# GpSimd rounds the rows in the first pass of the last feed-forward; VectorE keeps only the maxima

## The reference, cut to what matters

```
def quant_act_uint8(x):
    s = max(max(x), EPS) / 255.0            # one scale for the whole tensor
    return clip(round(x / s), 0, 255) * s, s

def quant_linear(x, w, b):                  # weights: int8, one scale per output row
    xq, s_in = quant_act_uint8(x)
    return xq @ wq.T + round(b / (s_in * s_w)) * (s_in * s_w)

x = x + quant_linear(relu(quant_linear(layernorm(x), w1, b1)), w2, b2)
```

## Time and profile before

| | |
|---|---|
| median of 3 executions | 2360.57 us (2360.05 to 2366.0) |
| profiled execution, its own time | 2361.02 us |
| span of its profile | 2359.2 us |
| TensorE busy | 2286.8 us, 97% |
| VectorE busy | 1743.7 us, 74% |
| ScalarE busy | 1587.5 us, 67% |
| GpSimd busy | 1691.7 us, 72% |
| first pass, first round to last maximum | 2250.78 to 2292.59 us |
| from there to the end of the span | 66.6 us |

### The profile page before, as it was taken

One profiled execution on the slowest core, in us unless ns is written; L12 is line 12 of the kernel. 1 busy time (PEld: TensorE's weight loads), 2 busy tenths in 40 slices (PEclk: granted clock), 3 DMA queues, 4 the chain that ended last, 5 costly groups with the idle time before them and its releaser, 6 DMA issues.

```text
span 2359.2 us, 62966 instructions
## 1 busy us (share of the span) xinstructions
PE 2286.8 (97%) x20874; PEld 1830.5 (78%) x20874; DVE 1743.7 (74%) x4342; ACT 1587.5 (67%) x4467; POOL 1691.7 (72%) x1863
## 2 busy tenths in 40 slices
PE   7999999999999999999999999999999999999788
PEld 6778877778788777778877778787777878877546
DVE  5777777787777777777777777777778777778785
ACT  6666666776667677666766766666677666667356
POOL 2777777777777777777787777777777777877607
PEclk9999999999999999999999999999999999999899
DMA  4000000000000000000000000000000000001202
GB/s 147 10 11 10 10 8 10 2 10 10 10 10 9 10 2 10 10 10 10 10 8 9 4 10 10 10 10 8 10 2 10 10 10 10 8 4 36 57 11 63
DMA packets 31472, 37.06 MB, mean 16 GB/s; under 512 B 3301, under 2 KB 29653, under 8 KB 31445
## 3 DMA queue, kind: packets, MB, share of 16 engines
q1 hardware_dynamic: 31444, 36.71, 5.3%
HBM read 29.36 MB, written 7.34 MB: 16 GB/s over the span
## 4 chain that ended last, share of the span: by engine, by line
PE 88%; DVE 4%; ACT 4%; issue 3%; POOL 2%; DMA 0%; POOLq 0%; ACTq 0%; SPq 0%; DVEq 0%
PE ps L367 25%; PE pt L471 11%; PE ps L447 10%; PE pa L483 7%; PE pt L461 5%; PE ps L411 5%; PE pa L523 4%; PE pa L498 4%; ACT probT L828 3%; PE ps L435 2%; PE pa L367 2%; PE pt L367 2%; PE pa L633 1%; PE ps L426 1%; DVE th L1547 1%
## 5 line engine op out<-in xcount | busy, mean ns | idle before, releaser
L1145 DVE TENSOR_REDUCE nmx<-ps 112x2 f32<-112x750 f32 x512 | 478.2, 934 | 142.2 <-PE ps L447 91.4
L1643 POOL TENSOR_TENSOR prob<-prob,rinv 112x375 f32<-112x375 f32 x512 | 404.2, 810 | 130.3 <-DVE rinv L1153 130.2
L1643 POOL TENSOR_TENSOR prob_last<-prob_last,rinv 112x375 f32<-112x375 f32 x512 | 411.9, 830 | 59.1 <-DVE rinv L1153 59.0
L828 ACT ACTIVATE room<-ps 128x376 f32<-128x376 f32 (+2 forms) x480 | 227.5, 487 | 265.9 <-PE ps L367 265.9
L828 ACT ACTIVATE probT<-pt 125x336 f32<-125x336 f32 (+1 forms) x512 | 242.6, 474 | 167.8 <-PE pt L461 112.5
L868 ACT ACTIVATE prob<-ps,nmx 112x375 f32<-112x375 f32 x512 | 289.9, 581 | 65.0 <-DVE nmx L1145 65.0
L868 ACT ACTIVATE prob_last<-ps,nmx 112x375 f32<-112x375 f32 x512 | 290.7, 584 | 8.2 <-DVE nmx L1145 8.2
L1670 POOL TENSOR_TENSOR krs<-krs,nhalf 125x48 f32<-125x48 f32 x32 | 257.0, 8030 | 0.0
L1136 DVE COPY probT<-pt 125x336 f32<-125x336 f32 x322 | 161.9, 503 | 97.4 <-PE pt L471 97.3
L483 PE MATMUL pa<-probT,room 125*64 125x112 f32 x3072 | 183.0, 265 | 0.0
L471 PEld LDWEIGHTS pt<-ident,prob 112*125 112x125 f32 x966 | 118.5, 189 | 72.7 <-issue 64.2
(11 more groups left out here) (294 smaller groups left out, 5981.0 us busy)
## 6 DMA issues: line engine op xcount, KB each, us to landing
craw<-in_ctx SPq DMA_DIRECT2D x32, 375.0 KB, 3.1
xin<-in_x SPq DMA_DIRECT2D x32, 112.0 KB, 2.0
x_rows<-x SPq DMA_DIRECT2D x32, 112.0 KB, 1.9
out<-probT SPq DMA_DIRECT2D x16, 224.0 KB, 2.3
room<-x_rows SPq DMA_DIRECT2D x1, 2576.0 KB, 13.7
w<-in_f1w SPq DMA_DIRECT2D x2, 1024.0 KB, 6.6
stage<-in_wk SPq DMA_DIRECT2D x2, 512.0 KB, 4.7
stage<-in_wv SPq DMA_DIRECT2D x1, 1024.0 KB, 7.5
```

The source lines that it names most:

```text
L828: return act.activation(dst, src, ACT.Copy)
L1145: top = dve.tensor_reduce(nmx[:, g:g + 2], ps[0:T, 2 * (i % 2):2 * (i % 2) + 2, 0:S], AX_X, ALU.max, negate=True)
L1643: pool.tensor_tensor(prob(i, n), prob(i, n), rinv[:, g:g + 1].to_broadcast([T, S]), ALU.mult).then_inc(s["normed"], 1)
```

## The change

The eight roundings leave VectorE's program and stand in GpSimd's, in one loop in front of the waits for the second pass. Each keeps its two waits, its operands, its operation and its counter. VectorE's program of the first pass is then the bias operations and 32 maxima in order. The waits of TensorE and ScalarE are unchanged.

```diff
-            def round_rows(c):
-                dve.wait_ge(s["xn3_ready"], c * CH + CH)
-                dve.tensor_scalar(xq3, x3n, ROUND, ROUND, ALU.add, ALU.subtract).then_inc(s["xq3_ready"], 1)
...
-            round_rows(0)
             link(dve.tensor_scalar(t8[:, 4, 0:FC], t8[:, 6, 0:FC], t8[:, 13, 0:1], None, ALU.mult))
             link(bias(t8[:, 4, 0:FC], f1b1[:], FC, t8[:, 5, 0:FC]))
-            def next_rows(c):
-                dve.wait_ge(s["xq3T_ready"], c + 1)
-                round_rows(c + 1)
-
             for c in range(NCH):
-                if 0 < c < NCH - 1:
-                    next_rows(c)
                 largest(c, 0)
                 largest(c, 1)
-                if c == 0:
-                    next_rows(c)
                 largest(c, 2)
                 largest(c, 3)
...
             pool.tensor_tensor(mr[:, B - 1:B, 1], mr[:, B - 1:B, 1], nhalf[0:T, 0:1], ALU.pow).then_inc(s["rstd3"], 1)
+            for c in range(NCH):
+                if c >= 1:
+                    pool.wait_ge(s["xq3T_ready"], c)
+                pool.wait_ge(s["xn3_ready"], c * CH + CH)
+                pool.tensor_scalar(xq3, x3n, ROUND, ROUND, ALU.add, ALU.subtract).then_inc(s["xq3_ready"], 1)
             pool.wait_ge(s["row_sb"], 2)
             pool.wait_ge(s["xq3_ready"], NCH)
```

## The result

The changed kernel took 2382.3 us (median of 4 executions, 2381.87 to 2384.33) against 2362.78 us before: ratio 1.0086, 95% interval 1.0073 to 1.0098. That is 19.5 us slower, past the 0.3% that can be told from no change and past the top of the range (2372). The profiled execution took 2382.22 us, its span is 2380.4, so again 1.8 us lie around it. The kernel before took 2361.05, 2361.29 and 2361.14 us in the larger sets of 7, 15 and 26 executions beside the experiments; against those the loss is 21 us. Two single executions among those of the experiments took 6433 and 6591 us; the ratios leave them out, and the profile that was taken of the second is not read.

What follows compares the result with a forecast made beforehand. VectorE was taken to bound the first pass at 4.60 us a chunk, the ring nearly tied at 4.44. With X = 1.45, 8X - 8.8 = +2.8 us on the 2360.57 median gave 2363.4 us, range 2358.8 to 2372.

Steps and rivals of the forecast that it cites:

- the ring: First pass, per chunk: round, transpose, copy, centre, round again; 4.44 us before the change, 3.75 us without the rounding.
- The formula: Growth of the first pass when all eight roundings move to GpSimd: 8X - 8.8 us, break-even at X = 1.10 us.
- X: GpSimd's time for one rounding plus its extra hand-over cost: put at 1.45 us, bounds 0.95 and 3.2.
- 6.7: Tail of the first pass: us from the start of the last transposes to the end of the last maximum.
- the write-only row: GpSimd memset of 1536 elements in 1377 ns; taken as lower bound, 0.95 us for 1024 with a little start.
- the repeated-value row: GpSimd two-input multiply, second input read as one repeated value; nearest upper bound, 1.95 us for 1024 elements.
- the far bound: Upper limit for X, 3.2 us: GpSimd's full two-input add extended to 1024 elements amid VectorE's work, 3.05, plus 0.16 hand-over.
- The second: Rival: GpSimd's rounding costs as much as two-input work or more, from X = 1.99; 2371 to 2377 us; chance 0.24.
- The clock: Rival: TensorE's clock falls as it waits about 1.5 us a turn in the first pass; +17 us; chance 0.02.
- Its contrary row: Evidence against a falling TensorE clock: from 2251 to 2260 TensorE was busy 5.93 of 9 us at clock 1.00.
- The rule that spoke against the change: Skill text on GpSimd: about 2 times slower with two inputs, +10 us; one input roughly line-rate, -0.4 us.

Runs made afterwards that it cites:

- Two buffers: The changed kernel with a second buffer each for centred and rounded rows and one more centring ahead on ScalarE, all eight roundings on GpSimd: 2359.35 us, ratio 0.9990.
- the control: The kernel before with second buffers for centred and rounded rows and one more centring ahead, all roundings on VectorE: 2361.16 us, ratio 0.9996.
- cast only: The changed kernel with GpSimd only casting the rows to bf16, the rounding left out: 2363.02 us, ratio 1.0002.
- one operation: The changed kernel with the subtraction left out of GpSimd's rounding, so the rows keep the added constant: 2376.04 us, ratio 1.0068.
- the change with TensorE kept busy: The changed kernel with ten useless matmuls ahead of each of the seven later transposes: 2382.22 us, ratio 1.0091; pass 64.6 us in a second run's trace.
- the kernel with GpSimd's operations by themselves: The kernel before with twelve extra GpSimd instructions on scratch rows behind GpSimd's last power, each waiting for the one ahead: 2370.46 us, one execution.

## Why the prediction was wrong

**What bounded the kernel, and what stood behind it: right.** VectorE bound the pass, and the ring through the single `x3n` and the single `xq3` took over at once. Its part outside the rounding is 3.75 us as read the earlier trace rows: 7.42 less 3.63 leaves 3.79, and the 0.04 more is the hand-over, where the rounding begins 0.16 us after the centring ends instead of 0.11 and the transposes 0.05 after it. Two buffers, which break the ring and leave the 3.63 us as they are, take the whole loss away, and the control shows that the buffers by themselves give only 1.2 us.

**The formula: right.** 8X - 8.8 us, against the growth of the pass: cast only X about 1.06, -0.3 for +1.6; one operation 2.81, +13.7 for +15.5; the change 3.67, +20.6 for +22.0; the change with TensorE kept busy 3.67, +20.6 for +20.4. What is missing in the first three, 1.4 to 1.9 us, lies in turns and tails whose transposes took 0.93 us, that is at the lower clock. In the changed kernel the last maximum ended 7.87 us after the last transposes began, not 6.7; with TensorE kept busy it was 6.63. Only there was the clock's part tested; in the other two it is read off the trace.

**The size of X: wrong, and this is the step that failed.** The sentence "it lies between the write-only row and the repeated-value row" set X at 1.45 us where 3.67 was measured. The rows for writes and for two-input adds priced the traffic; I took it for granted that one input cannot cost more than two. In GpSimd's case it does: 3.65 us for two operations on one input, 2.35 to 2.66 for one operation on two. Even the far bound, 3.2 us, came from that assumption. The nearest row was also not quite what it was taken for: the multiply of 768 elements repeats 48 values 16 times each (L1673), not one value, and with one value 1024 elements took 2.22 us, not 1.95. At 2.2 us over the value taken, eight times in a row, this term is 17.8 of the 18.9 us between the forecast of 2363.4 and the 2382.3 measured; the clock's 1.4 to 1.6 is the next. The two do not add up to 18.9 exactly, since the forecast started from 2360.57 us and the median of the kernel before moves by up to 2.2 us with the set of executions.

**The rivals.** The second, "costs as much as two-input work or more", is the one that happened; I gave it 0.24, and its price of 2371 to 2377 was too low. What spoke against it, that VectorE's maxima read PSUM, was right about contention: a rounding takes 3.65 us beside nothing but small operations and 3.63 beside the maxima. It was simply not where the cost lay. The clock, at 0.02 put too low, fell too, but it cost 1.6 us and not the 17 at which the rival was priced: it was down in part of the pass only (0.75 to 0.90 in stretches of 9 to 12 us), and the turn of about 7 us that the rival gave TensorE at half clock is no longer than the ring's 7.42. Its contrary row, 5.93 us busy of 9 at 1.00, did not carry over: 6.45 of 10 went with 0.76 here.

**The rule that spoke against the change.** The runs show how far each half of what the Trainium skill, "GPSIMD Engine Reference", section 4.1, says holds here. Copy and cast, 1.04 us for 1024 elements, agree with "roughly line-rate" for one input; arithmetic on one input does not, at 2.8 and 3.6 us. The factor of about 2 that the Trainium skill gives there is for two inputs; the rounding, with one, is 5.3 times VectorE's.

## What to carry to other kernels

Before an operation moves to another engine, write down the ring of waits that it is a link of: an engine relieved of 0.60 us a turn gains nothing if the slower engine's time goes into a ring that was only 0.16 us shorter. Buffers decide this; with a second buffer the same 3.63 us hid wholly, but for the first rounding, which nothing can cover. And take no price for an instruction form from rows of another form, fewer operands or not; where no row has it, the far bound must be left open, or the operation timed once by itself.

## What the hardware showed that I had not expected

On GpSimd, at 112 partitions x 1024 f32: copy or cast 1.04 us, tensor-scalar with one operation 2.77, with two 3.63 to 3.65; the output's width made no difference to copy and tensor-scalar.

While GpSimd works, VectorE's small operations between SBUF tensors can be held. In the changed kernel one begins 0.18 us after GpSimd's first rounding (2250.02 to 2253.68):

```profile
2250.00 0.17 DVE L1529 TENSOR_TENSOR t<-t 128x8 f32<-128x8 f32 x1
2250.20 0.89 DVE L1530 TENSOR_TENSOR t<-t 128x8 f32<-128x8 f32 x1
2251.13 0.17 DVE L1531 TENSOR_TENSOR t<-t 128x8 f32<-128x8 f32 x1
```

It was held for 0.7 us and not for the 3.5 us that the rounding still ran; the next one, with two SBUF inputs like it, took its usual 0.17 us beside the same GpSimd instruction. The hold does not go by the time that GpSimd's instruction takes. In all seven traces where GpSimd's first rounding or cast meets VectorE's bias operations, the one held ends 1.06 to 1.08 us after the start of the GpSimd instruction, whether that takes 1.04 us (the cast), 2.79 (one operation) or 3.64 to 3.66 (two). It may go by the width: the one such row beside 512 columns ended 0.68 us after the start (2252.91; 2253.12 + 0.47). In the kernel with GpSimd's operations by themselves the times beside 1024 columns were 1.07, 1.08 and, beside the instruction of 3.94 us, 1.37. In the cast-only kernel, GpSimd's line and VectorE's:

```profile
2250.87 1.04 POOL L1703 CAST hq<-hr 112x1024 bf16<-112x1024 f32 x1 [4.91 <-ACT hr L1052]
2250.89 1.04 DVE L1529 TENSOR_TENSOR t<-t 128x8 f32<-128x8 f32 x1
```

That is not the only place. In the kernel with the operations by themselves two tensor-scalars, begun 0.6 and 0.7 us before the end of a GpSimd instruction, end 0.03 us behind it (2252.25 + 0.61 against 2249.18 + 3.65, and 2259.39 + 0.69 against 2256.11 + 3.94). Why an instruction holds VectorE at its start and its end and not between stays open.

The Trainium skill, "SBUF — State Buffer", "Who interferes with whom", calls the ports that the two engines share an exclusive lock. It has a VectorE instruction with two SBUF inputs contend with a GpSimd one that reads SBUF, and says of VectorE's two-port modes that whoever issues first has the ports for the whole instruction. The rows show a contention, but in the changed kernel a shorter one than the instruction; the two tensor-scalars that end right behind GpSimd's instruction fit the whole of it. The sentence of the Trainium skill there that a reduction never contends agrees with the maxima at 1.087 us beside the roundings.
